# A layer norm that writes into the next stage's buffer on chip, with that stage's tables loaded during the norm

## The chip, the cores and the metric

The kernel runs on one core of a Trainium2 chip (trn2). The metric is the device time of one execution in microseconds, as the median of several runs. A core has TensorE (PE), VectorE (DVE), ScalarE (ACT), GpSimd (POOL) and SyncE (SP, whose own queue is written SPq), which run their own instruction streams and meet at semaphores, and 16 DMA engines.

## What is computed

The reference is a small vision tower: token selection, attention, a grouped-query block with a mixture of experts, a spectral filter and a tree of experts, with residual additions. The change touches the filter and the norm in front of it:

```python
h = h + _L1_attn_ref(_layernorm(h, axis=-1), L1_attn_eig_vals, L1_attn_eig_vecs, L1_attn_m_u, L1_attn_m_phi, L1_attn_m_y)

def _layernorm(x, axis=-1, eps=1e-05):
    m = jnp.mean(x, axis=axis, keepdims=True)
    v = jnp.var(x, axis=axis, keepdims=True)
    return (x - m) / jnp.sqrt(v + eps)
...
v_f = jnp.fft.rfft(eig_vecs, n=n, axis=0)
u_f = jnp.fft.rfft(inputs, n=n, axis=1)
conv = jnp.fft.irfft(v_f[None, :, :, None] * u_f[:, :, None, :], n=n, axis=1)[:, :l]
x_tilde = (conv * (eig_vals ** 0.25)[None, None, :, None]).reshape(b, l, k * d)
delta_phi = x_tilde @ m_phi
...
deltas = delta_phi + ar_u
...
out = jnp.einsum('okd,bkd->bo', m_y, carry) + delta_t
```

Here `ar_u` is the sum of three products of `m_u` with the tokens, shifted by 0, 1 and 2 places, and the last line is a recurrence over the tokens.

There are 4 sequences of 2049 tokens with 64 channels, all in float32.

## The kernel before

The program is a row of stages: `stage_select`, `stage_norm` "n0", `stage_attn`, norm "n1", `stage_gqa`, norm "n3", `stage_moe`, norm "n4", `stage_stu` (the filter), norm "n5", `stage_tree`. Each stage has its own buffers and semaphores (class `Room`), and closes with `clear_and_free_semaphores` and an `all_engine_barrier` (line 61), behind the end of its block (line 440 for a norm). So no engine starts a stage before all have ended the one before. Stages hand their results over in DRAM: n4 reads `h2` and writes `x_stu`, and `stage_stu` reads `x_stu`.

**The norm** holds the tokens as 128 partitions x 4098 columns: 64 channels of sequences 0 and 1 in the upper half, of 2 and 3 in the lower one, each half with its two sequences behind each other. SyncE loads them in 6 parts for each half (L445, with the averaging matrix at L447). It works on 11 chunks of 384 columns: TensorE averages (L470), VectorE subtracts (L528), GpSimd squares (L488), TensorE averages the squares (L473), ScalarE takes Ln and then Exp (L501, L504, six chunks and then five, with a table load at each change), and VectorE multiplies (L517). SyncE stores each part as its chunks are done (L457), and then waits for all stores.

**The filter's opening.** SyncE loads `eye`, waits for nine memsets of GpSimd (`NINIT`, L1959 to L1967), and then issues the tokens `U` (L1917), the small weights `tu` and `ty` (L1918, L1919), the eigenvectors (L1920), `lam` (L1922), the last tokens `ul` (L1924), the Fourier tables `F` (L1925) and the weights `M4` (L1927). `U` is a view of the second half of buffer `A`, and so its rows in the profile are called `stu_A`; in the same way the eigenvectors are `stu_G`. TensorE, ScalarE and VectorE wait for all 12 small loads (`small_loaded`), and ScalarE and VectorE also for the nine memsets. ScalarE then takes the roots of `lam` (L2126) and spreads the weights into `nat` (L2131, L2132). TensorE transposes them (L1984), transposes the tokens (L1991, copied out by ScalarE at L2140), computes ten blocks of direct products from `U` (L1997, in two banks in turn, copied out by VectorE at L2197), then the filter's spectrum from `F` (L2004) and the forward transforms (L2016). The main loop follows: `mix` (L2032) and `products` (L2048), with ScalarE and VectorE copying out the results of `mix` (L2158, L2236). VectorE's first instruction is the copy of `ul` into `uz` (L2194), and stands ahead of its copies of the direct blocks:

```python
dve.wait_ge(S["small_loaded"], 16 * NSMALL)
dve.wait_ge(S["init"], NINIT)
nc.vector.tensor_copy(uz[0:64, :], ul[0:64, :, 1]).then_inc(S["tail_ready"], 1)
for n, (p, o, w) in enumerate(WIN):
    dve.wait_ge(S["direct"], n + 1)
    nc.vector.tensor_copy(ACC[:, p, o:o + w], bank("direct", 0, n)[:, 0:w]).then_inc(S["direct_out"], 1)
```

The order on each engine is the order in which the code is written.

## Time and profile before

| | |
|---|---|
| median of 3 runs | 4077.76 us (4072.52 to 4079.02) |
| the profiled execution | 4077.61 us, span 4075.8 us |
| granted clock of TensorE, mean | 0.876 |
| busy: TensorE, VectorE, ScalarE, GpSimd | 79%, 66%, 56%, 17% |
| norm n4, first load to last product | 3014.8 to 3045.2 us |
| filter stage, first instruction to the next norm's first load | 3050.1 to 3494.3 us |

Times inside the execution count from the span's start. The span is a little shorter than the execution's own time. In rows, "idle before <-X" is how long the engine sat idle ahead of an instruction and what ended that idle time.

### The profile page before, as it was taken

The numbers are of one execution on the slowest core, as the hardware profiler recorded it, in microseconds if no ns is written. First come the engines' busy times: TensorE is split into PE (matmuls) and PEld (weight loads), VectorE is DVE, ScalarE is ACT, GpSimd is POOL, SyncE is SP. The second block draws the span as 40 slices with busy tenths as digits, with TensorE's granted clock in tenths as the row PEclk, the third lists the DMA queues.
The fourth block names the chain that finished last, engine by engine and source line by source line (L and its number), as shares of the span: only waits on it lengthen the run. The fifth ranks groups of instructions, "written<-read, shape, count | busy, mean of one in ns | idle before, by whom it ended". The sixth has DMA issues, their size and how long they took to land. (4 is left out here: it accounts for less than half of the span.)

```text
span 4075.8 us, 59841 instructions
## 1 busy us (share of the span) xinstructions
PE 3207.7 (79%) x21944; PEld 1563.4 (38%) x21945; DVE 2685.6 (66%) x4528; ACT 2264.3 (56%) x4775; POOL 702.4 (17%) x696
## 2 busy tenths in 40 slices
PE   7549999999999999747787888569977997443385
PEld 5323333333333333223344443322325775333253
DVE  1538999999999999748787877134432333346396
ACT  1138999999899999744565555423332330111243
POOL 1220111111111111120000000034420001102554
PEclk7559999999999999968898989679987899766698
DMA  2042001201100110030000000333323122630112
...
DMA packets 114669, 168.36 MB, mean 41 GB/s; under 512 B 67635, under 2 KB 92596, under 8 KB 106444
## 3 DMA queue, kind: packets, MB, share of 16 engines
...
q8 instruction: 167, 2.74, 0.3%
...
## 5 line engine op out<-in xcount | busy, mean ns | idle before, releaser
L1020 DVE TENSOR_REDUCE att_NM<-att_ring 121x1 f32<-121x1024 f32 x1088 | 1255.0, 1221 | 85.2 <-PE att_ring L860 84.4
L940 ACT ACTIVATE att_ring<-att_ring,att_NM 121x1024 f32<-121x1024 f32 x1088 | 1186.1, 1090 | 67.7 <-DVE att_NM L1020 64.1
L858 PE MATMUL att_ring<-att_q,att_k 64*121 64x512 f32 x2176 | 1142.5, 628 | 67.0 <-ACT att_ring L940 41.0
L860 PE MATMUL att_ring<-att_q,att_k 64*121 64x512 f32 x2176 | 1142.5, 628 | 0.0
L858 PEld LDWEIGHTS att_ring<-att_q,att_k 64*121 64x121 f32 x2176 | 330.3, 180 | 770.9 <-ACT att_ring L940 608.4
L1394 ACT ACTIVATE gqa_PT<-gqa_ring 121x484 f32<-121x484 f32 (+3 forms) x912 | 360.5, 451 | 203.2 <-PE gqa_ring L1321 136.3
L1438 DVE TENSOR_REDUCE gqa_NM<-gqa_ring 121x1 f32<-121x484 f32 (+1 forms) x720 | 375.3, 580 | 120.7 <-PE gqa_ring L1298 80.3
L860 PEld LDWEIGHTS att_ring<-att_q,att_k 64*121 64x121 f32 x2176 | 330.3, 180 | 0.0
L1321 PE MATMUL gqa_ring<-gqa_QS,gqa_KS 128*121 128x484 bf16 (+3 forms) x912 | 273.9, 332 | 36.0 <-ACT gqa_PT L1394 23.1
L1298 PE MATMUL gqa_ring<-gqa_KS,gqa_QS 128*121 128x484 bf16 (+1 forms) x720 | 253.4, 377 | 41.3 <-ACT gqa_PT L1394 19.2
L1778 DVE TENSOR_TENSOR moe_hh<-moe_sg,moe_p 128x484 f32<-128x484 f32 x204 | 134.4, 659 | 199.9 <-ACT moe_sg L1715 199.9
L1715 ACT ACTIVATE moe_sg<-moe_p 128x484 f32<-128x484 f32 x204 | 117.3, 575 | 218.2 <-PE moe_p L1672 218.2
L1672 PE MATMUL moe_p<-moe_fs,moe_W 64*64 64x484 f32 (+1 forms) x544 | 218.4, 610 | 18.7 <-POOL moe_xw L1625 18.7
L1673 PE MATMUL moe_p<-moe_xw,moe_W 64*64 64x484 f32 (+1 forms) x544 | 218.3, 609 | 0.0
L940 ACT ACTIVATION_READ_ACCUMULATOR att_ring<-att_ring,att_NM 121x1 f32 x1088 | 211.9, 195 | 0.0
L1335 PE MATMUL gqa_pA<-gqa_PT,gqa_V 121*32 121x484 f32 (+3 forms) x1824 | 185.8, 483 | 5.5 <-DVE gqa_YT L1472 4.9
L1321 PEld LDWEIGHTS gqa_ring<-gqa_QS,gqa_KS 128*121 128x121 bf16 x912 | 123.9, 146 | 163.0 <-ACT gqa_PT L1394 71.1
L717 POOL TENSOR_TENSOR att_pr<-att_q,att_k 128x2049 f32<-128x2049 f32 x16 | 72.2, 4512 | 606.9 <-PE att_ring L834 576.5
...
L1298 PEld LDWEIGHTS gqa_ring<-gqa_KS,gqa_QS 128*121 128x121 bf16 x720 | 103.3, 147 | 120.4 <-ACT gqa_PT L1394 37.9
L2587 ACT ACTIVATE tree_pq<-tree_pL,tree_xt 128x64 f32<-128x64 f32 x384 | 89.4, 316 | 108.0 <-DVE tree_both L2699 105.4
L1257 POOL COPY gqa_TK<-gqa_PB 121x128 bf16<-121x128 bf16 (+1 forms) x120 | 27.6, 278 | 696.2 <-DVE gqa_PB L1433 696.1
...
## 6 DMA issues: line engine op xcount, KB each, us to landing
...
moe_fs<-x_moe SPq DMA_DIRECT2D x4, 1028.5 KB, 10.7
...
```

Of the source, the lines that this page charges most:

```text
L858: nc.tensor.matmul(to[0:TT, 0:512], lo[0:64, par, TT * t:TT * t + TT], mlo[0:64, par, CK * ck:CK * ck + 512], start=True, stop=True)
L860: nc.tensor.matmul(to[0:TT, 512:1024], hi[64:128, par, TT * t:TT * t + TT], mhi[64:128, par, CK * ck + 512:CK * ck + 1024], start=True, st ...
L940: nc.scalar.activation(to[0:TT, :], to[0:TT, :], ACT.Exp, bias=NM[0:TT, turn % 2, g, ck:ck + 1], accum_out=SS[0:TT, turn % 2, g, ck:ck + 1 ...
L1020: nc.vector.tensor_reduce(NM[0:TT, turn % 2, g, ck:ck + 1], slot("score", turn, n)[0:TT, :], AX.X, ALU.max, negate=True).then_inc(S["max_r ...
L1298: ins = nc.tensor.matmul(to[0:T, 0:T * k], QS[:, par, h, T * t:T * t + T], KS[:, par, h // 2, GW * kg:GW * kg + T * k], start=True, stop=n ...
L1321: ins = nc.tensor.matmul(to[0:T, 0:T * k], KS[:, par, h // 2, T * s:T * s + T], QS[:, par, h, T * t0:T * (t0 + k)], start=True, stop=(s != ...
L1335: nc.tensor.matmul(pA[32 * i:32 * i + 32, o:o + T * k], V1[:, par, s, i // 2, :], PT[:, H * (n % QUADS) + i, 0:T * k], start=(s == 0), sto ...
L1394: nc.scalar.activation(PT[:, i % (QUADS * H), 0:T * k], bank("scores", n, h)[0:T, 0:T * k], ACT.Exp).then_inc(S["exped"], 1)
L1438: nc.vector.tensor_reduce(NM[:, u % 2, h, t % 4, kg:kg + 1], bank("maximum", n, 0)[0:T, 0:T * k], AX.X, ALU.max, negate=True).then_inc(S[" ...
L1672: nc.tensor.matmul(p1[cols, n % 3, 0:MC], W13[lo, g, cols], fs[lo, MC * i:MC * i + MC], start=True, stop=True).then_inc(S["up1"], 1)
L1673: nc.tensor.matmul(p3[cols, n % 3, 0:MC], W13[hi, g, cols], xw[hi, i % 3, :, e, :], start=True, stop=True).then_inc(S["up3"], 1)
L1778: nc.vector.tensor_tensor(hh[:, n % 4, :], sg[:, n % 3, :], p3[:, n % 3, 0:MC], ALU.mult).then_inc(S["hid_ready"], 1)
```

## The change

The filter stage now opens its buffers and semaphores first, and then calls the norm n4 itself, with three functions: `keep` (`into_u`) tells where each finished chunk goes in `U`, `next_loads` issues the filter's loads on SyncE behind the norm's own, and `next_fills` puts five of the nine memsets on GpSimd ahead of the norm's squares. The norm gets no output in DRAM (`outs` is empty), and neither stores nor waits for stores; the tensor `x_stu` is gone. In the filter, the tokens are not loaded, `ul` is copied from `U` by four small DMAs on chip with a semaphore of their own (`tail_loaded`) for which VectorE waits, and four memsets remain.

```diff
--- before.py
+++ after.py
@@ -385,7 +385,7 @@
 CH = 384
-def stage_norm(nc, name, h_in, outs, consts, kinds, weights):
+def stage_norm(nc, name, h_in, outs, consts, kinds, weights, keep=None, next_loads=None, next_fills=None):
@@ -448,6 +448,8 @@
                         for i, wt in enumerate(weights):
                             for side in range(2):
                                 sp.dma_start(w[64 * side:64 * side + 64, i:i + 1], wt.rearrange("(p a) -> p a", a=1)).then_inc(small_loaded, 16)
+                if next_loads:
+                    next_loads(sp)
                 for k, out in enumerate(outs):
                     for j, (c0, c1) in enumerate(cols):
                         sp.wait_ge(scaled, NC * k + min(2 * j + 2, NC))
@@ -455,7 +457,8 @@
                             e = c1 + out.shape[1] - B * N if side == 1 and j == PARTS - 1 else c1
                             sp.dma_start(out[:, 2 * side * N + c0:2 * side * N + e], T[k + 1][64 * side:64 * side + 64, c0:e]).then_inc(stored, 16)
-                sp.wait_ge(stored, 32 * PARTS * len(outs))
+                if outs:
+                    sp.wait_ge(stored, 32 * PARTS * len(outs))
             @block.tensor
             def _(pe):
@@ -474,6 +477,8 @@
             @block.gpsimd
             def _(pool):
+                if next_fills:
+                    next_fills(pool)
                 pool.wait_ge(padded, 1)
                 for s, (k, c) in enumerate(steps):
                     wait_input(pool, s)
@@ -513,7 +518,11 @@
                 def finish(s):
                     k, c = steps[s]
                     dve.wait_ge(inverted, s + 1)
-                    if kinds[k] == "ln":
+                    if keep:
+                        for to, part in keep(cut(c)):
+                            ins = nc.vector.tensor_tensor(to, T[k + 1][:, part], R[:, part], ALU.mult)
+                        ins.then_inc(scaled, 1)
+                    elif kinds[k] == "ln":
                         nc.vector.tensor_tensor(T[k + 1][:, cut(c)], T[k + 1][:, cut(c)], R[:, cut(c)], ALU.mult).then_inc(scaled, 1)
                     else:
                         j = kinds[:k].count("rms")
@@ -1819,28 +1828,79 @@
     with ExitStack() as ctx:
         r = Room(nc, ctx, "stu")
         eye = r.sb("eye", [128, 128])
...
         lam = r.sb("lam", [128, 4])
...
+        uz = r.sb("uz", [128, B])
+        A = r.sb("A", [128, 2, FH, 128])
...
+        U = A[:, 1, :, :].rearrange("a f o -> a (f o)")[:, 0:NP * UW].rearrange("a (p n) -> a p n", p=NP)
...
+        S = {n: r.sem(n) for n in names}
+        NSMALL, NEARLY, NINIT = 10, 5, 9
+        init = 0
+        def filled(pool, ins):
+            nonlocal init
+            init += 1
+            ins.then_inc(S["init"], 1)
+            pool.wait_ge(S["init"], init)
+        def early_fills(pool):
+            filled(pool, nc.gpsimd.memset(lam[:, :], 1.0))
+            filled(pool, nc.gpsimd.memset(nat[:, :, :], 0.0))
+            filled(pool, nc.gpsimd.memset(G[:, 0, 1, :], 0.0))
+            filled(pool, nc.gpsimd.memset(uz[:, :], 0.0))
+            filled(pool, nc.gpsimd.memset(U[:, :, 0:2], 0.0))
...
+        def early_loads(sp):
+            sp.dma_start(eye[:, :], consts[:, 0:128]).then_inc(S["small_loaded"], 16)
+            sp.wait_ge(S["init"], NEARLY)
+            for half in range(2):
+                q = slice(64 * half, 64 * half + 64)
+                sp.dma_start(tu[q, :], m_u.rearrange("o i a -> o (i a)")).then_inc(S["small_loaded"], 16)
+                sp.dma_start(ty[q, :], m_y.rearrange("o k d -> o (k d)")).then_inc(S["small_loaded"], 16)
+            sp.dma_start(ev, eig_vecs.rearrange("(a p) k -> p a k", p=128)).then_inc(S["small_loaded"], 16)
+            for j in range(4):
+                sp.dma_start(lam[32 * j:32 * j + K, 0:1], eig_vals.rearrange("(k a) -> k a", a=1)).then_inc(S["small_loaded"], 16)
+            sp.dma_start(F[:, :, :, :].rearrange("p a i f -> p (a i f)"), tables[:, 0:4096]).then_inc(S["dft_loaded"], 16)
+            for j in range(4):
+                sp.dma_start(M4[32 * j:32 * j + K, :, :], m_phi.rearrange("(k d) o -> k d o", k=K)).then_inc(S["mphi_loaded"], 16)
+        def into_u(cols):
+            parts = []
+            for p in range(NP):
+                c0, c1 = max(cols.start, N * p), min(cols.stop, N * (p + 1))
+                if c0 < c1:
+                    parts.append((U[:, p, 2 + c0 - N * p:2 + c1 - N * p], slice(c0, c1)))
+            return parts
+        stage_norm(nc, "n4", h_in, [], consts, ["ln"], [], keep=into_u, next_loads=early_loads, next_fills=early_fills)
...
-        uz = r.sb("uz", [128, B])
...
-        A = r.sb("A", [128, 2, FH, 128])
...
-        U = A[:, 1, :, :].rearrange("a f o -> a (f o)")[:, 0:NP * UW].rearrange("a (p n) -> a p n", p=NP)
         room = A[:, :, :, :].rearrange("a i f o -> a (i f o)")
         res = room[:, 0:NP * N].rearrange("a (p n) -> a p n", p=NP)
         at = NP * N
...
@@ -1910,21 +1963,9 @@
         with nc.Block() as block:
             @block.sync
             def _(sp):
-                sp.dma_start(eye[:, :], consts[:, 0:128]).then_inc(S["small_loaded"], 16)
-                sp.wait_ge(S["init"], NINIT)
-                for half in range(2):
-                    q = slice(64 * half, 64 * half + 64)
-                    sp.dma_start(U[q, :, 2:2 + N], u[:, 2 * half * N:(2 * half + 2) * N].rearrange("d (p n) -> d p n", p=NP)).then_inc(S["loaded"], 16)
-                    sp.dma_start(tu[q, :], m_u.rearrange("o i a -> o (i a)")).then_inc(S["small_loaded"], 16)
-                    sp.dma_start(ty[q, :], m_y.rearrange("o k d -> o (k d)")).then_inc(S["small_loaded"], 16)
-                sp.dma_start(ev, eig_vecs.rearrange("(a p) k -> p a k", p=128)).then_inc(S["small_loaded"], 16)
-                for j in range(4):
-                    sp.dma_start(lam[32 * j:32 * j + K, 0:1], eig_vals.rearrange("(k a) -> k a", a=1)).then_inc(S["small_loaded"], 16)
-                for half in range(2):
-                    sp.dma_start(ul[64 * half:64 * half + 64, :, :], u.rearrange("d (b n) -> d b n", b=B)[:, :, TAIL - 1:TAIL + 1]).then_inc(S["small_loaded"], 16)
-                sp.dma_start(F[:, :, :, :].rearrange("p a i f -> p (a i f)"), tables[:, 0:4096]).then_inc(S["dft_loaded"], 16)
-                for j in range(4):
-                    sp.dma_start(M4[32 * j:32 * j + K, :, :], m_phi.rearrange("(k d) o -> k d o", k=K)).then_inc(S["mphi_loaded"], 16)
+                for side in range(2):
+                    for half in range(2):
+                        sp.dma_start(ul[64 * half:64 * half + 64, 2 * side:2 * side + 2, :], U[64 * side:64 * side + 64, :, 1 + TAIL:3 + TAIL]).then_inc(S["tail_loaded"], 16)
                 sp.wait_ge(S["v_ready"], 2)
                 sp.dma_start(G[:, :, :, :].rearrange("p a i f -> p (a i f)"), tables[:, 4096:8192]).then_inc(S["inv_loaded"], 16)
                 for h in range(NH):
@@ -1949,23 +1990,11 @@
             @block.gpsimd
             def _(pool):
-                n = 0
-                def first(ins):
-                    nonlocal n
-                    n += 1
-                    ins.then_inc(S["init"], 1)
-                    pool.wait_ge(S["init"], n)
-                first(nc.gpsimd.memset(U[:, :, 0:2], 0.0))
-                first(nc.gpsimd.memset(lam[:, :], 1.0))
-                first(nc.gpsimd.memset(nat[:, :, :], 0.0))
-                first(nc.gpsimd.memset(G[:, 0, 1, :], 0.0))
-                first(nc.gpsimd.memset(uz[:, :], 0.0))
-                first(nc.gpsimd.memset(Xs[:, 0, :], 0.0))
-                first(nc.gpsimd.memset(ACC[:, :, N:NY], 0.0))
-                first(nc.gpsimd.memset(XF[:, :, :, :], 0.0))
-                first(nc.gpsimd.memset(V4[:, :, :], 0.0))
-                assert n == NINIT
+                filled(pool, nc.gpsimd.memset(Xs[:, 0, :], 0.0))
+                filled(pool, nc.gpsimd.memset(ACC[:, :, N:NY], 0.0))
+                filled(pool, nc.gpsimd.memset(XF[:, :, :, :], 0.0))
+                filled(pool, nc.gpsimd.memset(V4[:, :, :], 0.0))
+                assert init == NINIT
                 pool.wait_ge(S["resid"], 32)
                 pool.wait_ge(S["ends_out"], 2)
@@ -1982,7 +2011,6 @@
                 pe.wait_ge(S["nat_ready"], 4)
                 for a in range(5):
                     nc.tensor.transpose((pP[:, 0, 128 * a:128 * a + 128] if a < 4 else pP[:, 1, 0:128]), nat[:, a, :], eye[:, :]).then_inc(S["nat_turned"], 1)
-                pe.wait_ge(S["loaded"], 32)
                 for n in range(NP * NT // 4):
                     if n >= 4:
                         pe.wait_ge(S["u_turned_out"], n - 3)
@@ -2121,7 +2149,7 @@
             @block.scalar
             def _(act):
                 act.wait_ge(S["small_loaded"], 16 * NSMALL)
-                act.wait_ge(S["init"], NINIT)
+                act.wait_ge(S["init"], NEARLY)
                 nc.scalar.activation(lam[:, 1:2], lam[:, 0:1], ACT.Sqrt).then_inc(S["root"], 1)
                 act.wait_ge(S["root"], 1)
@@ -2191,6 +2219,7 @@
             def _(dve):
                 dve.wait_ge(S["small_loaded"], 16 * NSMALL)
                 dve.wait_ge(S["init"], NINIT)
+                dve.wait_ge(S["tail_loaded"], 64)
                 nc.vector.tensor_copy(uz[0:64, :], ul[0:64, :, 1]).then_inc(S["tail_ready"], 1)
                 for n, (p, o, w) in enumerate(WIN):
                     dve.wait_ge(S["direct"], n + 1)
@@ -2729,8 +2758,7 @@
     stage_gqa(nc, real(x_ln), real(x_rms), a["L0_ffn_wq"], a["L0_ffn_wk"], a["L0_ffn_wv"], a["L0_ffn_wo"], a["rope"], c, real(x_mid))
     stage_norm(nc, "n3", real(x_mid), [x_moe], c, ["rms"], [a["L0_ffn_ln2_w"]])
     stage_moe(nc, h1, x_mid, x_moe, a["L0_ffn_router_w"], a["L0_ffn_w1"], a["L0_ffn_w2"], a["L0_ffn_w3"], route_weights, c, h2)
-    stage_norm(nc, "n4", real(h2), [real(x_stu)], c, ["ln"], [])
-    stage_stu(nc, real(x_stu), real(h2), a["L1_attn_eig_vals"], a["L1_attn_eig_vecs"], a["L1_attn_m_u"], a["L1_attn_m_phi"],
+    stage_stu(nc, real(h2), a["L1_attn_eig_vals"], a["L1_attn_eig_vecs"], a["L1_attn_m_u"], a["L1_attn_m_phi"],
               a["L1_attn_m_y"], a["dft"], by_freq, c, real(h3))
     stage_norm(nc, "n5", real(h3), [x_tree], c, ["ln"], [])
     stage_tree(nc, x_tree, real(h3), a["L1_ffn_w1s"], a["L1_ffn_b1s"], a["L1_ffn_w2s"], a["L1_ffn_b2s"], a["tile_numbers"], c,
```

On SyncE, from the norm's first load to the filter's first tables. Before, with the stores (`x_stu<-n_T`) and the token loads (`stu_A<-x_stu`) between:

```order
L445 DMA n_T<-h 64x768 x2
L447 DMA n_mean<-in_consts 128x128
L445 DMA n_T<-h 64x768 x8
L445 DMA n_T<-h 64x258 x2
L457 DMA x_stu<-n_T 64x768 x10
L457 DMA x_stu<-n_T 64x258 x2
L440 UNCONDITIONAL_BRANCH
L1911 UNCONDITIONAL_BRANCH
L1913 DMA stu_eye<-in_consts 128x128
L1917 DMA stu_A<-x_stu 64x2x2049
L1918 DMA stu_tu<-in_L_attn_m_u 64x192
L1919 DMA stu_ty<-in_L_attn_m_y 64x128
```

And in the changed kernel:

```order
L445 DMA n_T<-h 64x258 x2
L1870 DMA stu_eye<-in_consts 128x128
L1874 DMA stu_tu<-in_L_attn_m_u 64x192
L1875 DMA stu_ty<-in_L_attn_m_y 64x128
L1874 DMA stu_tu<-in_L_attn_m_u 64x192
L1875 DMA stu_ty<-in_L_attn_m_y 64x128
L1876 DMA stu_G<-in_L_attn_eig_vecs 128x4x24
L1878 DMA stu_lam<-in_L_attn_eig_vals 24x1 x4
L1879 DMA stu_F<-in_dft 128x4096
L1881 DMA stu_M<-in_L_attn_m_phi 24x4096 x4
L440 UNCONDITIONAL_BRANCH
L1964 UNCONDITIONAL_BRANCH
```

All loads of small weights and tables moved ahead of the norm's end (the branch at L440); behind it only the four copies `stu_ul<-stu_A` are left ahead of the main loop.

On GpSimd, around the norm's squares (`n_SQ`), before:

```order
L488 TENSOR_TENSOR n_SQ<-n_T 128x384 x11
L440 UNCONDITIONAL_BRANCH
L60 ISA
L1950 UNCONDITIONAL_BRANCH
L1959 MEMSET stu_A 128x2x2
L1960 MEMSET stu_lam 128x4
L1961 MEMSET stu_nat 128x640
L1962 MEMSET stu_G 128x512
L1963 MEMSET stu_uz 128x4
L1964 MEMSET stu_Xs 128x128
L1965 MEMSET stu_ACC 128x2x8
L1966 MEMSET stu_XF 128x5120
```

And in the changed kernel:

```order
L1861 MEMSET stu_lam 128x4
L1862 MEMSET stu_nat 128x640
L1863 MEMSET stu_G 128x512
L1864 MEMSET stu_uz 128x4
L1865 MEMSET stu_A 128x2x2
L493 TENSOR_TENSOR n_SQ<-n_T 128x384 x11
L440 UNCONDITIONAL_BRANCH
L60 ISA
L1991 UNCONDITIONAL_BRANCH
L1993 MEMSET stu_Xs 128x128
L1994 MEMSET stu_ACC 128x2x8
L1995 MEMSET stu_XF 128x5120
```

Five memsets moved ahead of the squares.

On VectorE, in the norm, the products write into the filter's buffer, and the chunk across the boundary of two sequences is two instructions:

```order
L537 TENSOR_TENSOR n_T<-n_T,n_pS 128x384 x9
L523 TENSOR_TENSOR stu_A<-n_T,n_R 128x384 x5
L523 TENSOR_TENSOR stu_A<-n_T,n_R 128x129
L523 TENSOR_TENSOR stu_A<-n_T,n_R 128x255
L537 TENSOR_TENSOR n_T<-n_T,n_pS 128x384 x2
L523 TENSOR_TENSOR stu_A<-n_T,n_R 128x384 x4
L523 TENSOR_TENSOR stu_A<-n_T,n_R 128x258
```

Before, these were six and five products of 384 columns in the same two places.

## Rows read from the trace of the kernel before

**Rows 1.** Busy time by stretch; columns: stretch and length, busy us, PEclk, DMA share, GB/s.

```profile
3019.00:3024.00 5.00, 4.96 (x11) 2.92 (x12) 2.22 (x4) 0.00 (x0) 2.08 (x3) 0.69 1.00 258
...
3060.00:3070.00 10.00, 0.00 (x0) 0.00 (x0) 0.00 (x0) 0.00 (x0) 0.00 (x0) 0.50 1.02 211
...
3075.00:3080.00 5.00, 4.16 (x20) 4.19 (x21) 0.00 (x0) 3.38 (x9) 0.00 (x0) 0.50 0.89 292
3080.00:3085.00 5.00, 5.00 (x26) 3.33 (x25) 0.22 (x1) 2.87 (x6) 0.00 (x0) 0.99 0.78 167
```

**Rows 2.** Who waited for whom, 3040 to 3080: us in total, times, longest.

```profile
PE stu_pP L1984 <- ACT stu_nat L2132: 35.5, 1, 35.5
...
ACT stu_lam L2126 <- DMA stu_ul<-x_stu: 14.1, 1, 14.1
...
SPq L1917 <- POOL stu_V L1967: 8.1, 1, 8.1
...
SPq L440 <- DMA x_stu<-n_T: 1.8, 1, 1.8
```

**Rows 3.** Timeline, the norm's end; columns: start us, us, engine, line, instruction.

```profile
3042.78 2.43 DVE L517 TENSOR_TENSOR n_T<-n_T,n_R 128x384 f32<-128x384 f32 x5 [5.97 <-ACT n_R L504]
...
3043.84 3.65 SPq L457 DMA_DIRECT2D x_stu<-n_T  x6
```

**Rows 4.** Timeline, the filter's memsets and loads.

```profile
3050.15 0.10 POOL L1959 MEMSET stu_A<- 128x4 f32 x1 [12.11 <-POOLq L61]
...
3051.90 0.20 POOL L1964 MEMSET stu_Xs<- 128x128 f32 x1
...
3056.76 1.80 POOL L1967 MEMSET stu_V<- 128x2048 f32 x1
3058.59 0.63 SPq L1917 DMA_DIRECT2D stu_A<-x_stu  x1
...
3059.27 0.60 SPq L1918 DMA_DIRECT2D stu_tu<-in_L_attn_m_u  x1
...
3064.85 1.27 SPq L1924 DMA_DIRECT2D stu_ul<-x_stu  x2
...
3066.82 1.70 SPq L1927 DMA_DIRECT2D stu_M<-in_L_attn_m_phi  x4
```

**Rows 5.** Timeline, ScalarE's first computation in the filter and VectorE's first direct copy.

```profile
3058.64 1.28 ACT L2126 ACT_TABLE_LOAD   x1 [14.24 <-POOL stu_V L1967]
...
3074.06 0.20 ACT L2126 ACTIVATE stu_lam<-stu_lam 128x1 f32<-128x1 f32 x1 [14.13 <-DMA stu_ul<-x_stu]
...
3084.78 0.69 DVE L2197 COPY stu_ACC<-stu_pS 128x512 f32<-128x512 f32 x1 [10.56 <-PE stu_pS L1997]
```

**Rows 6.** Timeline, the norm's opening.

```profile
3016.60 6.20 SPq L445 DMA_DIRECT2D n_T<-h  x10
...
3019.04 4.36 PE L470 MATMUL n_pS<-n_T,n_mean 128*128 128x384 f32 x8 [8.27 <-DMA n_mean<-in_consts]
...
3021.56 0.83 POOL L488 TENSOR_TENSOR n_SQ<-n_T 128x384 f32<-128x384 f32 x1 [35.46 <-DVE n_T L528]
```

**Rows 7.** DMA, 3050 to 3090: traffic in 40 slices; an issue, KB, us to landing.

```profile
GB/s 0 66 0 0 0 0 0 0 0 25 180 303 180 229 165 201 257 205 197 192 164 263 246 279 426 442 426 295 164 131 197 147 197 164 131 164 33 0 0 0
...
stu_F<-in_dft SPq DMA_DIRECT2D x1, 2048.0 KB, 12.4
```

**Rows 8.** The main loop: ScalarE's copies on the timeline, and two stretches as in rows 1.

```profile
3171.82 1.92 ACT L2158 COPY stu_A<-stu_pA 128x1024 f32<-128x1024 f32 x1 [2.85 <-PE stu_pA L2032]
3181.38 1.98 ACT L2158 COPY stu_A<-stu_pA 128x1024 f32<-128x1024 f32 x1 [2.46 <-PE stu_pA L2032]
3188.95 1.96 ACT L2158 COPY stu_A<-stu_pA 128x1024 f32<-128x1024 f32 x1 [2.45 <-PE stu_pA L2032]
...
3170.00:3175.00 5.00, 5.00 (x123) 4.26 (x116) 1.96 (x1) 2.41 (x2) 0.00 (x0) 0.50 0.63 122
3180.00:3185.00 5.00, 5.00 (x139) 4.72 (x134) 2.39 (x3) 2.41 (x2) 0.00 (x0) 1.00 0.03 7
```

29 lines of the change are left out of this document (14 added, 15 removed).

## The prediction, made before the result was known

> **What bounds the kernel now.** The kernel is a row of stages with a full stop between two of them, so only the stretch that the diff touches has to be read: the norm n4, the stop behind it, and the opening of the filter stage. I read first the busy time by stretch. From 3060 to 3070 no engine computes at all, while the DMA engines are at a share of 1.02; TensorE is back in 3075 to 3080 [rows 1]. The table of waits shows how long the hole is and what fills it: TensorE waits 35.5 us (from the norm's end, about 3040.3) for ScalarE's copy of the weights (`stu_nat`), ScalarE itself 14.1 us for a DMA (the last of the small loads), and on SyncE's own queue 1.8 us go to the norm's last store and 8.1 us to GpSimd's last memset (`stu_V`) [rows 2]. So in this hole nothing computes and three things follow each other: stores, memsets, loads.
>
> The timeline gives their ends. VectorE finishes the norm at 3042.78 + 2.43 = 3045.21. SyncE's last store is issued by 3043.84 + 3.65 = 3047.49 [rows 3], and 1.8 us later, at 3049.3, it has landed [rows 2]. The filter stage's first instruction runs at 3050.15 [rows 4], so the stop between the stages costs 0.85 us. GpSimd's nine memsets run from 3050.15 to 3056.76 + 1.80 = 3058.56, and SyncE, which waits for them, issues the token load at 3058.59 and the last of the small loads, the two of `stu_ul`, from 3064.85 [rows 4]. ScalarE's first computation starts at 3074.06 [rows 5]: 15.5 us behind the first load. From there on the stage is bound by TensorE: 5.00 of 5 us busy in 3080 to 3085 [rows 1].
>
> **The change, part by part.**
>
> 1. Stores of the norm go. VectorE writes its last product into the filter's buffer. What ends the norm is then VectorE at 3045.21 and not a landing at 3049.3: 4.1 us less. The product for the chunk across the sequence boundary is two instructions (129 and 255 columns) in place of one of 384, and the last one has 258 columns and not 384. Five products lie in 2.43 us [rows 3], 0.49 each, so the extra one costs 0.1 to 0.5 us, and it stands ahead of two subtractions for which GpSimd and TensorE wait; the narrower one gives back up to 0.2 us at the end. I take 0 for the pair, with -0.2 to +0.5 for the range.
>
> 2. The filter's wait for its memsets goes. From 3050.15 to 3058.59 is 8.4 us. Five of the nine (`lam`, `nat`, `G`, `uz`, the halo of `U`) now stand on GpSimd ahead of the norm's squares. They took from 3050.15 to 3051.90, 1.75 us [rows 4]; the norm's first square starts only at 3021.56, and the norm's fourth load is issued at 3016.60 already [rows 6], so GpSimd has at least 5.0 us for 1.8 us of work. Cost nothing; without that cover 1.8 us. The other four stay where they are, and take 3051.90 to 3058.56, 6.7 us, for VectorE alone (see 4).
>
> 3. The loads go to the norm. Of the 15.5 us between first load and first computation, one piece stays: ScalarE's table load, 1.28 us, which now lies open, since it ended long before the data came in [rows 5]. With 0.08 us ahead of it that is 1.36 us, so 14.1 us go. The cover is the norm. SyncE is free at 3016.60 + 6.20 = 3022.80, when the norm's own 13 loads are issued [rows 6]. The issues from `tu` at 3059.27 to `M4`'s end at 3066.82 + 1.70 = 3068.52 take 9.25 us; without the second token load (0.65) and `ul` (1.3) that is 7.3 us, and 0.4 for `eye` [rows 4], so the last table is issued at 3030.5, `M4`'s first at about 3028.8 and `F` at about 3028.2. `F` landed 12.4 us after its issue, with the token load ahead of it, and DMA traffic ended at 3086 [rows 7], 19.2 us after `M4`'s first issue. So `F` lands by 3040.6, `M4` by 3048.0. `F` is read first for the filter's spectrum, after the ten output blocks of the direct products; `M4` later still. The small loads were issued ahead of `F` and are in by 3037. Nothing of the norm stands behind them: SyncE has no store left, and its 12 token loads are ahead in the queue. The price is nothing, with 0 to 0.5 us for a norm that shares its memory with 3.5 MB of traffic.
>
> 4. A wait is added. VectorE waits for four small copies on chip (`ul` from `U`), then copies `uz`, and behind this stand its ten copies of the direct blocks; TensorE, with two banks, waits for the first of them ahead of its third block. The copies are issued within 4 x 0.63 = 2.5 us of the stage's start and landed in 2.5 us at the norm's small stores, so at +5 us; GpSimd's four memsets end at +6.7 us, and VectorE is ready at about +7. The first direct block was finished at 3084.78, 10.7 us after ScalarE's start at 3074.06 [rows 5], thus +12.1 us in the new count. Cover of 5 us: cost nothing. If the copies were later than +12, every us more would count.
>
> The row of DMA traffic bears on this: behind `F`'s landing at 3078.6 it goes on at 131 to 197 GB/s up to 3086, less than half of the 426 to 442 just ahead [rows 7]. The Trainium skill, DMA: Bandwidth & Descriptors, "Why a DMA increments its semaphore by 16 and not by 1", says that a copy is spread over the largest number of engines up to 16 that divides its slowest dimension, which for the 24 partitions of `M4` would be 8; and "Queues, rings and completion order" says that an engine takes its descriptors in ring order. The trace agrees with the half rate. By that rule the four small copies would stand behind `M4`, that is behind 3048.0, which is the rival B below.
>
> **The sum.** Before, ScalarE starts at 3074.06. After: 3045.21 + 0.85 (stop) + 1.36 (table load) = 3047.42. The difference is 26.6 us (4.1 + 8.4 + 14.1). From ScalarE's start on, both versions have the same order on every engine, and what follows is a chain of stages, so nothing is late next and all of it should reach the end. The profiled execution took 4077.61 us with a span of 4075.8, so 4051.0 and a span of 4049.2; it lies 0.15 us below the median of the runs, which gives 4051.2. I take 4051.1. By the bounds of parts 1 and 3 and a stop of up to 2 us the gain is 24.5 to 26.8.
>
> **The rivals.**
>
> A. The stop waits for the tables. No row shows a stage that ends with loads in flight. If the stop, or the fetch of the filter's code, had to wait until the 3.5 MB are in, the filter would start at 3048.0 to 3049 and not 3046.1: the gain is 23.7 to 24.7, about 4053.5. Against it: SyncE's row names as its last wait a store it asked for itself [rows 2]. Chance 0.10.
>
> B. The small copies come late, behind `M4`'s rest. They are then in 2.5 us after 3048.5, at 3051, and VectorE is only needed at 3058.2. It costs only if `M4` ran past 3055, 7 us longer than its 19.2 us before; then perhaps 3 us, 4054. Chance 0.04.
>
> C. TensorE's clock steps fall elsewhere in the filter. The granted clock moves between 0.50 and 1.00 through the stage: it is 0.50 in 3170 to 3175 and 1.00 in 3180 to 3185, and the step between two of ScalarE's copies takes 9.6 us (3171.82 to 3181.38) at mostly the low one and 7.6 us (to 3188.95) at the high one [rows 8]. So each such step that changes sides is 2 us. The stage's opening does not change: TensorE comes out of its pause at 0.50 in both versions, and the clock rises after some 4 us of work, in the norm (0.69 in 3019 to 3024) as here (0.50 in 3075 to 3080, 0.99 in the next 5 us) [rows 1]; 0.50 is 1.2 GHz, 1.00 is 2.4. Three steps either way are 6 us: 4045 or 4057. Chance 0.16, half on each side; the three runs of before, 6.5 us apart, show that such shifts exist.
>
> D. The clock stays low after the shorter pause (9 us in place of 35). Then the TensorE-bound work up to `mix`, 3080 to 3125 before, takes twice its 45 us, and the time is 4077.8 - 26.6 + 45 = 4096, slower than before. It decides once 35 us of full-clock work run at half (26.6 + 8.2). Against it: in the norm the clock rose after a pause of 8.27 us [rows 1, 6]. Chance 0.02.
>
> E. The gain is mostly given back by something not seen, such as norm steps held up by the tables' traffic by 20 us: no row for it, VectorE's steps keep their 0.49 us while stores run. Within 0.2%: 0.02.
>
> **How the numbers follow.** The forecast has 0.66: 4051.1, itself good for 4048 to 4054, with the scatter of runs. The range takes in A, B and C: 4045 to 4058; outside lie D, E and the tails, under 2 in 10. The 0.2% that a measurement of this kernel can tell from no change are 8.2 us; every case but D and E is faster by more than that: faster 0.96, same 0.02, slower 0.02.
>
> **What would show it.** In the new profile: the filter stage's first memset 0.85 us behind VectorE's last norm product; ScalarE's table load right behind it, and no wait for a DMA at its first computation; TensorE idle for some 9 us and not 35; VectorE's `uz` copy about 7 us into the stage and its first direct copy still released by TensorE; no step of the norm longer. If the stop takes more than 2 us, A is right; if TensorE waits for VectorE at the third direct block, B; if the opening gains 26.6 us and the end does not, C.

## The result

| | kernel before | changed kernel |
|---|---|---|
| median of 4 runs each | 4075.14 us (4072.49 to 4079.02) | 4044.97 us (4037.17 to 4046.48) |
| the profiled execution | 4077.61 us, span 4075.8 | 4046.48 us, span 4044.7 |
| granted clock of TensorE, mean | 0.876 | 0.877 |
| n4's first load to its last product's end | 30.4 us | 31.9 us |
| last product's end to the filter's first instruction | 4.94 us | 0.77 us |
| filter's first instruction to ScalarE's first computation | 23.91 us | 1.36 us |

The ratio is 0.9921, with a 95% interval of 0.9905 to 0.9937, which stands for about 32 us. The medians are 30.2 us apart where 26.6 were forecast, from a base that the fourth run of the kernel before moved from 4077.76 to 4075.14. 4044.97 lies just below the range, 4045 to 4058.

The mechanism is the forecast one. This is the timeline of the changed kernel at the end of the norm and the opening of the filter (start, busy us, engine and line; in brackets the idle time ahead and what ended it; `...` stands for lines left out):

```profile
3036.99 1.28 ACT L509 ACT_TABLE_LOAD   x1
3038.28 2.17 ACT L509 ACTIVATE n_R<-n_R 128x384 f32<-128x384 f32 x5
3038.83 2.30 DVE L523 TENSOR_TENSOR stu_A<-n_T,n_R 128x384 f32<-128x384 f32 x5 [5.97 <-ACT n_R L509]
3041.90 2.66 SPq L1968 DMA_DIRECT2D stu_ul<-stu_A  x4
3041.90 0.20 POOL L1993 MEMSET stu_Xs<- 128x128 f32 x1 [7.82 <-POOLq L61]
3041.97 1.28 ACT L2154 ACT_TABLE_LOAD   x1 [1.51 <-PEq L61]
...
3043.26 0.20 ACT L2154 ACTIVATE stu_lam<-stu_lam 128x1 f32<-128x1 f32 x1
...
3045.05 1.30 PE L2013 MATMUL stu_pP<-stu_eye,stu_nat 128*128 128x128 f32 x5 [8.70 <-ACT stu_nat L2160]
...
3048.66 0.16 DVE L2223 COPY stu_uz<-stu_ul 64x4 f32<-64x4 f32 x1 [7.53 <-POOL stu_V L1996]
...
3054.48 0.69 DVE L2226 COPY stu_ACC<-stu_pS 128x512 f32<-128x512 f32 x1 [5.66 <-PE stu_pS L2025]
```

Against the same places of before [rows 3 to 5]: the last products write `stu_A` (that is `U`) and not `n_T`; the filter starts 0.77 us behind them, with no store between; ScalarE's table load, hidden before, is the 1.28 us ahead of its first computation; and no DMA ends a wait any more. TensorE was idle for 8.70 us where it was 35.5 [rows 2]. VectorE comes to its `uz` copy 6.8 us into the stage, released by GpSimd's last memset and not by the small copies, and its first copy of a direct block stands 12.6 us into the stage, released by TensorE.

Two of its stretches (busy us and count for PE, PEld, DVE, ACT, POOL, then granted clock, DMA share, GB/s), to be read against [rows 1]:

```profile
3045.00:3050.00 5.00, 4.95 (x24) 4.98 (x25) 0.16 (x1) 3.15 (x7) 3.51 (x2) 0.50 0.03 3
3050.00:3055.00 5.00, 5.00 (x23) 3.22 (x23) 0.52 (x1) 2.44 (x5) 0.00 (x0) 0.96 0.00 0
```

TensorE comes back at 0.50 (1.2 GHz) and is at 0.96, near 1.00 (2.4 GHz), in the next 5 us, after 8.7 us of pause as after 35 before. The clock did not stay low. The tables' issues, and the DMA traffic from 3009 to 3049 in 40 slices of 1 us:

```profile
3022.70 0.35 SPq L1879 DMA_DIRECT2D stu_F<-in_dft  x1
...
3023.10 1.73 SPq L1881 DMA_DIRECT2D stu_M<-in_L_attn_m_phi  x4
...
GB/s 0 77 308 185 283 215 255 255 258 244 225 65 79 3 180 164 410 442 393 442 328 156 147 180 131 213 147 131 180 33 0 0 0 0 2 2 1 0 0 0
...
stu_F<-in_dft SPq DMA_DIRECT2D x1, 2048.0 KB, 8.0
```

`F` landed 8.0 us after its issue, at 3030.7 (9.3 to 9.5 us in the three repeats of this kernel), and `M4`'s traffic ended at about 3038.5: 3.4 us before the filter opened. So in this kernel the stop never met a load in flight, and the four small copies met no queue. Neither rival A nor rival B could show here; both have an experiment of their own below.

Where the 31.1 us between the two spans arose (4075.8 - 4044.7): n4 starts at 3009.24 and not at 3014.82, in code that is the same in both, which is 5.58 us. From n4's first load to the filter's first spectrum product (`stu_pP` from `stu_F` and `stu_G`) are 64.70 us and not 89.42: 24.72 us, the change itself. From there to the end, 970.76 us and not 971.56: 0.80. So the profiled pair has less in the changed part than forecast, and more from outside it.

### The profile page after: what moved, and what is told of

The parts are those of the page before. It is cut to its first block and busy times, and to the rows that moved or that the text cites. A ratio compares the mean times of both kernels' runs of the same rounds, so it can differ in the third digit from the quotient of the medians.

```text
span 4044.7 us, 59830 instructions
## 1 busy us (share of the span) xinstructions
PE 3211.7 (79%) x21944; PEld 1563.9 (39%) x21945; DVE 2684.7 (66%) x4529; ACT 2261.7 (56%) x4775; POOL 702.4 (17%) x696
## 5 line engine op out<-in xcount | busy, mean ns | idle before, releaser
L1307 PE MATMUL gqa_ring<-gqa_KS,gqa_QS 128*121 128x484 bf16 (+1 forms) x720 | 252.9, 376 | 40.8 <-ACT gqa_PT L1403 19.2
L1681 PE MATMUL moe_p<-moe_fs,moe_W 64*64 64x484 f32 (+1 forms) x544 | 218.1, 609 | 18.7 <-POOL moe_xw L1634 18.7
L1307 PEld LDWEIGHTS gqa_ring<-gqa_KS,gqa_QS 128*121 128x121 bf16 x720 | 103.2, 146 | 119.8 <-ACT gqa_PT L1403 37.8
```

Source lines behind the costliest of these rows:

```text
L1307: ins = nc.tensor.matmul(to[0:T, 0:T * k], QS[:, par, h, T * t:T * t + T], KS[:, par, h // 2, GW * kg:GW * kg + T * k], start=True, stop=n ...
L1681: nc.tensor.matmul(p1[cols, n % 3, 0:MC], W13[lo, g, cols], fs[lo, MC * i:MC * i + MC], start=True, stop=True).then_inc(S["up1"], 1)
```

## Experiments

Each difference below is against the changed kernel unless it says otherwise.

**1. How far the two kernels repeat.** The kernel before and the changed kernel again, unedited, the latter twice.

> The kernel before, unchanged, to see how far two executions of one program differ stage by stage. Theory 1 (the change is worth 26.6 us at the filter's opening, and the other 3 to 5 us of the measured difference are scatter of stages that it does not touch): the median lies in 4072 to 4079 us, ratio 1.000; the new profile differs from the first one by 2 to 5 us in the grouped-query stage (861.7 us from norm to norm before), in the filter behind its first transpose (418.5 us) and in the last stages (581.5 us), together with the granted clock of the stretch, and by under 0.3 us from n4's first load to the filter's first memset apart from clock steps (35.3 us). Theory 2 (the change makes something else faster too, such as the grouped-query stage or the tree stage by another place of the DRAM tensors): this profile repeats 861.7, 418.5 and 581.5 us within 1 us each.

> The changed kernel, unchanged. Theory 1: the ratio to the kernel before is 1 - 26/4076 = 0.9936, with single runs 3 to 6 us around it; n4's first load to the first transpose of the filter takes 34.5 to 36 us again (61.0 before), and the other stages scatter as in the kernel before. Theory 2: the ratio is 0.992 or lower again, with the grouped-query stage at 857 us and the last stages at 577 us again.

> The changed kernel once more, for the stages that it does not touch. In two profiles of it the last stages (from the load of norm n5 to the end) took 577.4 and 578.7 us, in four of kernels with a later filter 581.5 to 582.1, and TensorE's wait for the second token load of the tree stage 52 us and 53 to 56. Theory 1 (scatter): this profile and those of the three kernels beside it spread from 577 to 582 us. Theory 2 (something systematic gives 4 us there): all four take 577 to 579 us.

Measured: `before_again` 4074.94 us over 11 runs (4071.30 to 4083.69), ratio 0.9995 (0.9986 to 1.0004). `after_again` 4047.75 over 6, one of them 6600.26, at a granted clock of 1.000, for a reason that no run shows; it is left out of all that follows, and the median without it is 4046.01; ratio 0.9926 (0.9913 to 0.9939). `after_third` 4052.02 over 4 (4046.55 to 4055.11), ratio 0.9938 (0.9923 to 0.9953), with the kernel before at 4078.20. So by their ratios three batches give gains of about 32, 30 and 25 us for the same pair, and by their medians 30.2, 30.3 and 26.2. All 14 runs of the changed kernel have their median at 4046.2 and their mean at 4047.0 (scatter of one run 4.6), the 50 of the kernel before 4076.3 and 4076.4 (3.5). The difference of the means is 29.4, give or take 2.7 (twice 4.6/sqrt(14) and 3.5/sqrt(50), added in squares). The change's own part, from n4's first load to the spectrum, scatters much less: 89.4 to 90.6 us in six profiles in which that stretch is the kernel before, 63.1 to 64.7 in seven in which it is the changed one (those of experiment 6 are among them), means 90.21 and 63.46. That is 26.75 us, give or take some 0.5, where 26.6 were forecast; single pairs give 24.7 to 27.5.

**2. Only the buffer: tokens kept on chip, tables and memsets where they were.**

```diff
-        stage_norm(nc, "n4", h_in, [], consts, ["ln"], [], keep=into_u, next_loads=early_loads, next_fills=early_fills)
+        stage_norm(nc, "n4", h_in, [], consts, ["ln"], [], keep=into_u)
...
             def _(sp):
+                early_loads(sp)
...
             def _(pool):
+                early_fills(pool)
```

(with SyncE and ScalarE waiting for all nine memsets, as before).

> The norm writes into the filter's token buffer and stores nothing, but all loads and all nine memsets stay at the filter's opening. Theory 1: the filter's first memset comes 4.1 us earlier against n4's first load (31.2 us and not 35.3), the memsets keep their 8.4 us, and ScalarE starts when the last small load has landed, some 7.5 us behind the first one and not 15.5, since no token load of 1 MB stands ahead. So 12 us of gain, 4064 us. The four small copies of the last tokens now stand behind 3.5 MB of tables: if they wait for them, VectorE's first copy of a direct block is held by them and not by TensorE, and 0 to 3 us are lost. A rival says that the stores were hidden and the gain of this part is nothing: 4076.

Measured: 4066.84 us over 10 runs, ratio 0.9977 (0.9967 to 0.9986). The stretch up to the spectrum takes 84.3 us, 5.9 less than before. The opening of the stage, from the timeline:

```profile
3054.15 0.35 SPq L1879 DMA_DIRECT2D stu_F<-in_dft  x1
3054.55 1.77 SPq L1881 DMA_DIRECT2D stu_M<-in_L_attn_m_phi  x4
...
3056.36 2.65 SPq L1969 DMA_DIRECT2D stu_ul<-stu_A  x4
...
3063.60 5.32 PE L2027 MATMUL stu_pS<-stu_A,stu_tr 128*128 128x512 f32 x12
3072.53 0.16 DVE L2225 COPY stu_uz<-stu_ul 64x4 f32<-64x4 f32 x1 [32.39 <-DMA stu_ul<-stu_A]
3072.61 1.27 DVE L2228 COPY stu_ACC<-stu_pS 128x512 f32<-128x512 f32 x2
3073.34 8.80 PE L2027 MATMUL stu_pS<-stu_A,stu_tr 128*128 128x512 f32 x17 [4.43 <-DVE stu_ACC L2228]
```

The stretch behind the stop, in the columns of rows 1:

```profile
3073.00:3078.00 5.00, 4.66 (x6) 2.08 (x7) 0.89 (x2) 0.00 (x0) 0.00 (x0) 0.50 0.00 0
```

Its DMA traffic from 3040 to 3080, in slices of 1 us:

```profile
GB/s 0 7 59 0 0 0 0 0 0 0 48 50 66 49 0 262 262 459 426 393 459 198 197 131 98 197 197 180 147 66 19 0 0 0 0 0 0 0 0 0
```

This is rival B at work, and the 12 us expected were missed. Four copies of 1 KB each, on chip, issued at 3056.36, are there at 3072.5, 16.2 us later; the traffic of `F` and `M4`, issued just ahead of them, ends at about 3071. VectorE's `uz` copy waits for them, its copies of the direct blocks stand behind that, TensorE fills its two banks and stops, ahead of the third block. The stop is 4.43 us, and the direct products then run at the low clock (0.50 in 3073 to 3078, where the changed kernel has 1.00 from 3055 on): from the first direct product to the spectrum are 3093.47 - 3063.60 = 29.87 us, in the changed kernel 3073.94 - 3051.70 = 22.24. So 7.6 us are lost for one stop of 4.4. The rest of the account: the stores' 4.1 us, and 9.6 us because no token load stands ahead of the small ones any more (ScalarE computes 5.86 us behind the first of them, 3049.36 to 3055.22, and not 15.5). 4.1 + 9.6 - 7.6 is 6.1, measured 5.9. The Trainium skill, DMA: Bandwidth & Descriptors, "Queues, rings and completion order", has an engine take its descriptors in ring order, and "Why a DMA increments its semaphore by 16 and not by 1" leaves a copy whose slowest dimension is 24 with 8 engines. The trace agrees with the first: the small copies land when the traffic ahead has ended, and of the packets under 512 bytes 160 run in 3060 to 3062, as `F` ends, 35 in the next 7 us and 445 from 3069 on. It agrees with the second in that the traffic behind `F` is slower; but it is at less than half, 98 to 198 GB/s after 393 to 459, so whether the 8 engines are all of it is not shown.

**3. Only the time of the loads: tables, weights and five memsets in the norm, tokens still over DRAM.**

```diff
-        stage_norm(nc, "n4", h_in, [], consts, ["ln"], [], keep=into_u, next_loads=early_loads, next_fills=early_fills)
+        stage_norm(nc, "n4", h_in, [u], consts, ["ln"], [], next_loads=early_loads, next_fills=early_fills)
...
-                for side in range(2):
-                    for half in range(2):
-                        sp.dma_start(ul[64 * half:64 * half + 64, 2 * side:2 * side + 2, :], U[64 * side:64 * side + 64, :, 1 + TAIL:3 + TAIL]).then_inc(S["tail_loaded"], 16)
+                for half in range(2):
+                    q = slice(64 * half, 64 * half + 64)
+                    sp.dma_start(U[q, :, 2:2 + N], u[:, 2 * half * N:(2 * half + 2) * N].rearrange("d (p n) -> d p n", p=NP)).then_inc(S["loaded"], 16)
```

(and `ul` from DRAM, as before).

> The small loads, tables and five memsets are moved into the norm, but the tokens still go over DRAM: the norm stores them and the filter loads them (2 x 512 KB) as its first DMAs. Theory 1: the filter's first instruction comes where it came before, 35.3 us behind n4's first load; ScalarE starts 1.36 us later; TensorE transposes the weights at 3.1 us, and then waits for the tokens, which land 6 to 8 us into the filter. Before, the same transposes of tokens began 26.6 us into the filter, so the gain is 19 to 20 us: 4057. If the wait for the memsets had been the whole price, it would be 8 us.

Measured: 4064.34 us over 4 runs, ratio 0.9963 (0.9948 to 0.9977). The stretch up to the spectrum takes 77.4 us, 12.8 less than before, where 19 to 20 were expected. The timeline:

```profile
3049.29 1.28 SPq L1968 DMA_DIRECT2D stu_A<-x_stu  x2
...
3052.43 1.30 PE L2015 MATMUL stu_pP<-stu_eye,stu_nat 128*128 128x128 f32 x5 [14.58 <-ACT stu_nat L2163]
...
3062.04 5.02 PE L2022 MATMUL stu_pA<-stu_eye,stu_A 128*128 128x128 f32 x32 [8.30 <-DMA stu_A<-x_stu]
```

and one line of its transfers, from 3005 to 3065 (KB of one, us from issue to landing):

```profile
x_stu<-n_T SPq DMA_DIRECT2D x10, 192.0 KB, 7.7
```

Two things took the difference. The tokens (1 MB in each of two loads, not the 512 KB of the expectation) are there 12.75 us after the first issue (3049.29 to 3062.04), where I had allowed 6 to 8. And the norm's stores, now behind the tables on the same queue, take 7.7 us from issue to landing where they took 3.0 in the kernel before, so that n4's first load to the filter's first instruction is 37.5 us, against 35.3 to 36.1 in the kernel before. The two halves of the change alone are worth 5.9 + 12.8 = 18.7 us, together 26.75: each takes away what the other would run into. With the tokens on chip there is no store for the tables to delay and no load at the opening; with the tables early the small copies find an empty queue.

**4. Loads in flight over the stop.** SyncE issues `F` and `M4` only when the norm's last product is done.

```diff
-        def early_loads(sp):
+        def early_loads(sp, scaled, last):
...
+            sp.wait_ge(scaled, last)
             sp.dma_start(F[:, :, :, :].rearrange("p a i f -> p (a i f)"), tables[:, 0:4096]).then_inc(S["dft_loaded"], 16)
```

> The changed kernel, but SyncE issues the tables F and M4 only when the norm's last product is done, so that 3.5 MB are in flight while the stages change. Theory 1 (the stop between stages does not wait for loads): the filter's first memset again 0.8 us behind VectorE's last product. The rival (it waits for them): the filter starts 15 us later, since F and M4 took 15.5 us from issue to the end of the traffic. The four small copies of the last tokens then stand behind M4, as in the run with all loads at the filter's opening, and land some 17 us into the filter instead of 5; TensorE needs VectorE at 15 us (third direct block), so 2 to 4 us are lost against the changed kernel: ratio 0.994 where the changed kernel has 0.993, and 0.9965 by the rival.

Measured: 4055.38 us over 4 runs, ratio 0.9942 (0.9927 to 0.9958). The timeline, and the transfers of 3040 to 3075:

```profile
3044.44 0.35 SPq L1880 DMA_DIRECT2D stu_F<-in_dft  x1
3044.84 1.81 SPq L1882 DMA_DIRECT2D stu_M<-in_L_attn_m_phi  x4
3047.62 2.66 SPq L1969 DMA_DIRECT2D stu_ul<-stu_A  x4
3047.63 0.20 POOL L1994 MEMSET stu_Xs<- 128x128 f32 x1 [10.27 <-POOLq L61]
3047.69 1.28 ACT L2155 ACT_TABLE_LOAD   x1 [3.97 <-PEq L61]
...
3062.57 0.16 DVE L2224 COPY stu_uz<-stu_ul 64x4 f32<-64x4 f32 x1 [18.15 <-DMA stu_ul<-stu_A]
...
3063.37 5.98 PE L2026 MATMUL stu_pS<-stu_A,stu_tr 128*128 128x512 f32 x18 [0.88 <-DVE stu_ACC L2227]
...
stu_F<-in_dft SPq DMA_DIRECT2D x1, 2048.0 KB, 8.1
```

Rival A falls in this form. The last table is issued by 3046.65, the filter starts 0.97 us later, and `F` landed at 3052.5, `M4`'s traffic ended at about 3061. This stop did not wait for the loads in flight, nor did the fetch of ScalarE's tables: its 1.28 us are the same. What shows in its place is rival B in small: the small copies land 14.9 us behind their issue, with the end of the traffic, VectorE's first copy of a direct block stands 15.0 us into the stage and not 12.6, and TensorE waits 0.88 us for it. The spectrum comes 66.6 us after n4's first load and not 63.5; 1.9 us of that is the issues that SyncE still had to make behind the last product (n4's first load to the filter's first instruction is 33.7 us, against 31.8 as the mean of the seven profiles of the changed kernel), and 1.2 the direct products, which take 23.4 us up to the spectrum and not 22.2.

**5. Is what remains of the opening worth anything?** In the first kernel the roots of `lam`, and so the table load, stand behind ScalarE's copies of the transposed tokens; in the second GpSimd also spreads the weights into `nat`, in the norm, behind its last square.

```diff
-                nc.scalar.activation(lam[:, 1:2], lam[:, 0:1], ACT.Sqrt).then_inc(S["root"], 1)
-                act.wait_ge(S["root"], 1)
-                nc.scalar.activation(lam[:, 2:3], lam[:, 1:2], ACT.Sqrt).then_inc(S["lam_ready"], 1)
...
+                nc.scalar.activation(lam[:, 1:2], lam[:, 0:1], ACT.Sqrt).then_inc(S["root"], 1)
+                act.wait_ge(S["root"], 1)
+                nc.scalar.activation(lam[:, 2:3], lam[:, 1:2], ACT.Sqrt).then_inc(S["lam_ready"], 1)
```

```diff
+                if next_spread:
+                    pool.wait_ge(squared, len(steps))
+                    next_spread(pool)
```

> The changed kernel, with ScalarE's two roots of lam, and so the table load of 1.28 us, moved behind its copies of the weights and of the transposed tokens; VectorE needs the roots 30 us later. By theory 1 TensorE's first transpose comes 1.4 to 1.5 us into the filter and not 3.15, so the gain against the changed kernel is 1.7 us; the end moves by that, which is less than the scatter of single runs: 4045. A rival: the copies themselves need the table load, or the moved one delays the tokens' copies, and nothing changes.

> As the one before, and the four copies that spread the weights are done by GpSimd behind its last square in the norm, where it is idle for 7.8 us. Theory 1: TensorE's first transpose comes at once, 0.1 to 0.3 us into the filter, 3 us earlier than in the changed kernel, and ScalarE has only its copies of the results left: 4044. Rival: GpSimd's copies of 64 x 192 with a stride take over 2 us each and hold the end of the norm, so that the gain is nothing.

Measured: 4050.33 us over 5 runs, ratio 0.9930 (0.9917 to 0.9944), and 4046.70 over 5, ratio 0.9925 (0.9912 to 0.9939). TensorE's first transpose on the timeline, of the first and of the second:

```profile
3048.86 1.30 PE L2013 MATMUL stu_pP<-stu_eye,stu_nat 128*128 128x128 f32 x5 [7.09 <-ACT stu_nat L2157]
```

```profile
3040.28 1.30 PE L2025 MATMUL stu_pP<-stu_eye,stu_nat 128*128 128x128 f32 x5 [5.78 <-PEq L61]
```

They stand 1.53 and 0.21 us into the stage, against 3.15, as expected. ScalarE starts its copies 0.07 us into the stage in both, without a table load ahead. The spectrum comes 61.7 and 58.5 us after n4's first load, and 63.5 in the changed kernel. Of that difference 0.6 and 2.0 us lie in the norm, ahead of the stage (in the second it took 29.06 us, against 30.8 to 31.9), so that 1.1 and 3.0 us are the stage's own. So the opening did get shorter, by 1.7 and 5.0 us, and the end shows neither: the forecasts of 4045 and 4044 us were missed, and both intervals hold the ratio of the changed kernel itself as well as one that is 1.7 or 5.0 us better. These runs can't say whether what is left of the opening is worth anything at the end.

**6. The part that nobody touched.** From n5's first load to the end the first three profiles of the changed kernel took 577.4, 578.7 and 578.9 us, and two of the kernel before 581.5 and 581.9. The difference is there by the fourth group of products of the tree stage (`tree_pL`, eight in a group): it starts 115.6 to 121.7 us behind n5's first load, and from it to the end are 460.1 to 462.2 us in all eighteen profiles. SyncE's loads for the third and the fourth group, and TensorE's wait for them at the third, in the changed kernel and then in `before_again`:

```profile
3571.35 0.85 SPq L2423 DMA_DIRECT2D tree_xs<-x_tree  x1
3573.07 0.59 SPq L2423 DMA_DIRECT2D tree_xs<-x_tree  x1
...
3578.37 3.76 PE L2519 MATMUL tree_pL<-tree_W,tree_xs 128*121 128x255 f32 x8 [51.97 <-DMA tree_xs<-x_tree]
```

```profile
3600.56 0.51 SPq L2394 DMA_DIRECT2D tree_xs<-x_tree  x1
3601.76 0.59 SPq L2394 DMA_DIRECT2D tree_xs<-x_tree  x1
...
3609.99 3.73 PE L2490 MATMUL tree_pL<-tree_W,tree_xs 128*121 128x255 f32 x8 [55.79 <-DMA tree_xs<-x_tree]
```

The same wait is 7.0 us behind the first load's issue in one and 9.4 in the other. Both kernels were run once more, and then with a GpSimd memset ahead of n5's loads, which delays all that follows; its width is the only thing that differs between the three kernels of each kind, so their instructions are the same in number and order.

```diff
             def _(sp):
+                if name == "n5":
+                    sp.wait_ge(held, 1)
...
             def _(pool):
+                if name == "n5":
+                    nc.gpsimd.memset(R[:, 0:2048], 0.0).then_inc(held, 1)
```

(2048 in the shifted kernels, 16 and 4096 in the held ones.)

> The changed kernel once more, for the last stretch alone: from the next norm's first load (n5) to the end of the span, code that the change does not touch. It took 577.4, 578.7 and 578.9 us in the three profiles of the changed kernel, and 581.5 and 581.9 in the two of the kernel before. If the shorter stretch belongs to the program as it is, this profile gives 577 to 579 again. If it is chance, drawn anew in each execution from 577 to 583, any value there is as likely, and one above 580.5 settles it.

> The kernel before once more, for the last stretch alone (n5 to end): 581.5 to 582 if its length belongs to the program, anything from 577 to 583 if it is chance.

> The changed kernel with a GpSimd memset of 2048 columns (1.8 us) ahead of the loads of the norm behind the filter, so that everything from there on starts about 1.9 us later. If the length of the last stretch depends on where it falls in time against something that runs on by itself, it changes here from 577 to 579 to another value, 580.5 to 583 by the other profiles. If it belongs to the program, it stays at 577 to 579. If it is chance, it says nothing by itself but will not go with the kernel.

> The kernel before with the same memset of 1.8 us ahead of the loads of the norm behind the filter. By place in time, the last stretch comes out at another value than 581.5 to 582. By program it stays there. By chance it is anything from 577 to 583.

> As after_shifted, with the memset cut from 2048 to 16 columns: the same instructions in number and order, and 1.7 us less of delay. After_shifted had 580.2 us from the norm's first load to the end, against 577.4 to 578.9 in four profiles of the changed kernel without the memset. If the length goes with the program's text, this one has 580.2 again. If it goes with the place in time, it is back at 577.4 to 578.9, since nothing else is delayed.

> As after_shifted, with a memset of 4096 columns: the same instructions, 1.8 us more of delay. By the program's text 580.2 us for the last stretch again. By the place in time a value of its own, by the profiles so far anywhere from 576.6 to 582.9.

> As before_shifted, with the memset cut from 2048 to 16 columns. Before_shifted had 576.6 us for the last stretch, against 581.5 to 582.4 in three profiles of the kernel before without the memset. By the program's text 576.6 again; by the place in time back at 581.5 to 582.4.

> As before_shifted, with a memset of 4096 columns, 1.8 us more of delay. By the program's text 576.6 us for the last stretch again; by the place in time another value, 577.5 to 582.9.

Measured, one execution each, n5's first load to the end, in us:

| memset ahead of n5 | kernel before | changed kernel |
|---|---|---|
| none | 581.5, 581.9, 582.4 | 577.4, 578.7, 578.9, 578.2 |
| 16 columns | 581.6 | 581.2 |
| 2048 columns | 576.6 | 580.2 |
| 4096 columns | 578.6 | 578.7 |

The executions took 4044.90, 4043.74, 4050.85 and 4053.48 us (changed: none, 2048, 16, 4096) and 4074.68, 4071.34, 4071.20 and 4082.20 (before, in the same order). With the same instructions the stretch took 576.6 to 581.6 us in one kernel and 578.7 to 581.2 in the other, so its length doesn't go with the program. Nor is it fixed by the delay: 16 columns delay nothing worth naming, and yet the changed kernel was at 581.2 there. The kernel before with 2048 columns, which had the shortest stretch:

```profile
3596.94 0.78 SPq L2399 DMA_DIRECT2D tree_xs<-x_tree  x1
3598.58 0.59 SPq L2399 DMA_DIRECT2D tree_xs<-x_tree  x1
...
3602.45 3.76 PE L2495 MATMUL tree_pL<-tree_W,tree_xs 128*121 128x255 f32 x8 [47.95 <-DMA tree_xs<-x_tree]
```

That is 5.5 us behind the first load's issue, and the issue came at 103.9 us behind n5's first load, 1.8 to 3.3 us earlier than in the three unedited ones. Over the eighteen profiles that wait ends 5.0 to 11.5 us behind the first load's issue; the issue itself stands 103.2 to 107.2 us behind n5's first load, and the fourth group 5.6 to 7.7 us behind the third. What they vary with, these runs don't say. The four and the three unedited profiles fall into two groups that don't overlap, and I can't call that chance with confidence; but the kernel before left its group when it was delayed by 1.8 us, the changed one with 16 columns already, and the five kernels of experiments 2 to 5, whose code from n5 on is the same, had 580.8 to 582.9 us.

## Why the prediction was right, and where it was wrong

Each of the first four points is held against the step of the same number.

1. **Stores.** Right. The norm's end is the last product, and the stop follows 0.77 us behind it, forecast 0.85. Alone, with the loads where they were, the buffer is worth 5.9 us, in which these 4.1 are one of three terms.

2. **Memsets.** Right. The five early ones end 1.7 us behind n4's first load, 5.1 us before the first square.

3. **Loads.** Right in its sum: ScalarE computes 1.36 us into the stage, to the hundredth. The tables came sooner than I had them: `F` in 8.0 us (9.3 to 9.5 in the repeats) and not 12.4, with no token load ahead, and the traffic's end 15.4 us behind `M4`'s first issue and not 19.2. The norm of the profiled changed kernel took 1.5 us more than that of before, because TensorE's first eight products took 5.49 us where it had been 4.36 [rows 6], at 0.50 in 3014 to 3019. That looked like a price of the tables' traffic, but the tables were not yet issued then, and the repeats take it away: 30.4, 31.0 and 31.1 us for the norm of the kernel before, 31.9, 30.9, 30.9 and 30.9 for that of the changed one.

4. **Small copies.** Right: cover enough, and no cost. What I had underrated is what they cost if the cover goes. Rival B had "perhaps 3 us"; the second experiment shows 7.6 us for a stop of 4.4, because TensorE goes back to the low clock (0.50 for the next 5 us).

**The sum.** 26.6 forecast, 26.75 measured over thirteen profiles, for the part that the change touches; that they meet to 0.15 us is in part luck, since the mean itself is good to some 0.5. The terms hold one by one too: the stop comes 4.1 us sooner (forecast 4.1), and from the stage's start to ScalarE's first computation are 1.36 us and not 24.1, in the mean of the six (22.7, forecast 22.5). As far as the scatter lets one see, it reached the end: the pooled gain is 29.4, give or take 2.7.

**The step that failed** is the last one: "4051.1, itself good for 4048 to 4054, with the scatter of runs". Its base was the median of three runs, 4077.76, and the profiled 4077.61 beside it. Their agreement to 0.15 us said nothing: the next run was 4072.49, which puts the base 2.6 us lower, and 50 runs have their median at 4076.3. The profiled execution had 3014.82 us ahead of n4; over the eighteen profiles, whose code up to there is the same, that number goes from 3006.7 to 3016.1. Of the 6.1 us between 4051.1 and 4044.97, by the means of all runs, 1.3 are this base, 2.8 the pooled gain over the forecast one, and 2.0 the four measured runs, which lay lower than the fourteen. From the three runs of before, 6.5 us apart, I had the scatter in hand, and put it into rival C as a small chance instead of into the forecast. With 3.5 and 4.6 us for a single run, a base of three runs and a result of four miss by 3.1 us as means (3.5/sqrt(3) and 4.6/sqrt(4), added in squares), and by a quarter more as medians; twice that is 7 to 8 us to each side of 4051 even with everything else right, where I had 3, and the range had to reach 4043 or 4044 below. Over 14 runs the changed kernel is at 4046.2, inside the range, so that the miss by 0.03 us is itself a matter of chance.

**Rival C** named a mechanism, the clock's steps, and put it in the filter's main loop. That stretch does differ: from the spectrum to n5's first load are 389.9 to 396.7 us over the eighteen profiles, 390.1 and 393.3 in the first pair, so here the changed kernel lost 3.2 us. But other untouched stretches differ as much: between n1's first load and n3's there are 853.2 to 862.1 us over the eighteen profiles, eight of them within 853.2 to 853.7, six within 856.9 to 857.2, three within 861.7 to 862.1 and one at 858.6. There the granted clock goes with the length: 0.88 in the fourteen up to 857.2 us, 0.87 in the four above; which of the two sets the other is not shown. From the spectrum to the end there are 971.6, 975.1 and 975.2 us in the unedited kernel before and 970.8 to 971.6 in the unedited changed one. Whether the 2.6 us by which the pooled gain (29.4, give or take 2.7) exceeds 26.75 are anything but scatter is open: the interval just reaches it, and the last stretch of experiment 6 would be the place for it.

**A** is refuted by the fourth experiment. **D** did not come: the clock rose after the pause of 8.7 us. (C gives "some 4 us of work" ahead of the rise for the norm too; there the granted clock was 0.50 up to 3022 and 0.94 in the next 1 us, and TensorE's first product stands at 3019.04.) **E** did not come: nothing like 20 us was given back.
